# Gated cross-attention and mixture of experts on one core: SyncE's queue writes the query parts ahead of the key reads, and sends the query reads and the reciprocals ahead of the row of maxima

## What is computed

```python
q = proj(x1t, Wq, bq);  k = proj(x2t, Wk, bk);  v = proj(x2t, Wv, bv)
scores = jnp.einsum('bhqd,bhkd->bhqk', q, k) / sqrt(16)
out = jnp.einsum('bhqk,bhkd->bhqd', softmax(scores), v)
...
x = x + jnp.tanh(g_xattn[0]) * attention(_layernorm(x), ctx)
x = x + jnp.tanh(g_ffn[0]) * moe_and_shared_ffn(_layernorm(x))
```

## Time and profile before

| | us |
|---|---|
| median of 3 runs | 1412.91 |
| lowest and highest run | 1408.93, 1428.1 |
| the profiled execution | 1411.02 |
| its span (first to last instruction) | 1409.1 |
| PE busy | 1290.6 (92%) |
| DVE busy | 974.3 (69%) |
| ACT busy | 874.1 (62%) |
| POOL busy | 863.3 (61%) |
| mean granted TensorE clock, of full speed | 0.982 |

### The profile page before, as it was taken

One profiled execution on the slowest core, in us unless ns is written; L12 is line 12 of the kernel. 1 busy time (PEld: TensorE's weight loads), 2 busy tenths in 40 slices (PEclk: granted clock), 3 DMA queues, 4 the chain that ended last, 5 costly groups with the idle time before them and its releaser, 6 DMA issues.

```text
span 1409.1 us, 34589 instructions
## 1 busy us (share of the span) xinstructions
PE 1290.6 (92%) x12274; PEld 680.4 (48%) x12274; DVE 974.3 (69%) x1661; ACT 874.1 (62%) x1720; POOL 863.3 (61%) x1267
## 2 busy tenths in 40 slices
PE   2899899999998899889999988799999999999997
PEld 0233333333333333323333332387788878888885
DVE  4988889999987798888889887556654323333332
ACT  2488788888877788778878876534334333333332
POOL 8547677767787687867787752640214555555553
PEclk7799999999999999999999999999999999999999
DMA  6567777777777677677777664376654888886565
GB/s 177 166 175 212 205 215 210 206 211 193 194 207 191 187 194 197 189 187 208 192 196 193 196 164 112 122 209 145 126 176 90 203 197 202 198 190 112 111 108 80
DMA packets 161348, 248.28 MB, mean 176 GB/s; under 512 B 33733, under 2 KB 58956, under 8 KB 161182
## 3 DMA queue, kind: packets, MB, share of 16 engines
q1 hardware_dynamic: 142926, 208.70, 53.5%
q0 software_dynamic: 18256, 37.38, 14.5%
HBM read 141.06 MB, written 103.88 MB: 174 GB/s over the span
## 4 chain that ended last, share of the span: by engine, by line
PE 42%; DMA 13%; SPq 12%; issue 12%; POOL 9%; DVE 9%; ACT 2%; POOLq 1%; DVEq 0%; another core or an unknown queue 0%; ACTq 0%
PE m_banks L969 19%; SPq L471 7%; PE bank L926 6%; PE bank L895 6%; DVE row_max L1142 6%; PE m_banks L873 4%; DMA arena<-pv_d 4%; DMA arena<-parts_q 4%; DMA parts_k<-arena 3%; PE bank L901 2%; POOL xs L793 2%; SPq L532 2%; PE bank L857 1%; PE bank L851 1%; PE bank L991 1%
## 5 line engine op out<-in xcount | busy, mean ns | idle before, releaser
L1142 DVE TENSOR_REDUCE row_max<-m_banks 128x2 f32<-128x1024 f32 x512 | 614.8, 1221 | 98.5 <-PE m_banks L873 89.7
L1426 ACT ACTIVATE arena<-bank 128x512 f32<-128x512 f32 x1024 | 554.4, 605 | 97.7 <-PE bank L895 89.9
L895 PE MATMUL bank<-arena 112*32 112x512 bf16 x4096 | 338.2, 384 | 11.9 <-ACT arena L1426 7.2
L926 PE MATMUL bank<-arena 128*32 128x512 f32 x2048 | 283.2, 603 | 1.9 <-issue 1.6
L895 PEld LDWEIGHTS bank<-arena 112*32 112x32 bf16 x4096 | 113.1, 95 | 275.5 <-ACT arena L1426 136.3
L873 PE MATMUL m_banks<-arena 48*128 48x512 bf16 x1024 | 176.6, 391 | 58.2 <-DMA arena<-parts_q 29.2
L805 POOL DMA_INDIRECT out<-xs,ids x71 | 112.3, 1581 | 172.9 <-ACT xs L1508 140.7
L969 PE MATMUL m_banks<-w_ring,h_hi 128*128 x568 | 183.0, 403 | 0.0
L1497 ACT ACTIVATE arena<-m_banks 128x256 f32<-128x256 f32 x103 | 39.5, 384 | 189.7 <-PE m_banks L969 179.3
L873 PEld LDWEIGHTS m_banks<-arena 48*128 48x128 bf16 x1024 | 40.3, 94 | 194.7 <-issue 83.2
L694 POOL TENSOR_TENSOR arena<-arena 128x512 f32<-128x512 f32 x32 | 40.9, 1279 | 122.8 <-DMA arena<-pv_d 119.4
(11 more groups left out here) (182 smaller groups left out, 1997.9 us busy)
## 6 DMA issues: line engine op xcount, KB each, us to landing
pv_d<-arena SPq DMA_DIRECT2D x32, 512.0 KB, 4.4
w_ring<-split_d SPq DMA_DIRECT2D x60, 256.0 KB
parts_k<-arena SPq DMA_DIRECT2D x96, 128.0 KB
parts_q<-arena SPq DMA_DIRECT2D x96, 128.0 KB
arena<-parts_k SPq DMA_DIRECT2D x64, 192.0 KB
arena<-parts_q SPq DMA_DIRECT2D x64, 192.0 KB
arena<-in_w SPq DMA_DIRECT2D x36, 256.0 KB, 7.2
arena<-in_ctx SPq DMA_DIRECT2D x32, 256.0 KB, 3.7
```

Source lines behind the costliest of these rows:

```text
L895: last = nc.tensor.matmul(out[c, :], k_stack[b % 3][0:SHIFTED, h, kt * P + c.start:kt * P + c.stop], q_stack[b % 3][0:SHIFTED, h, :], star ...
L926: last = nc.tensor.matmul(pv_ps[2 * DH * j:2 * DH * (j + 1), :], v_ones[b % 3][:, kt, GROUP * g + j, :], probs[pair % 3][:, j, :], start=( ...
L1142: nc.vector.reduce_max(pair, m_ps[(STEPS * b + u) // 2 % M_PAIRS], AX_X).then_inc(s_mx, 1)
L1426: nc.scalar.activation(probs[group % 3][:, j, :], bank_of["scores", b, s], ACT.Exp, scale=float(DH) ** -0.5).then_inc(s_exp, 1)
```

## The change

In every turn SP now issues the writes of query MID and LO ahead of the key reads. The query reads come right behind `load_x`, then `store_reciprocals`, and `row(i+1, 0)` last, just ahead of `load_values`. No DMA is added or removed, and no wait is added or removed in the program; only the order in SP's program is another. For batch 0 (i = -2) the writes stood ahead of the key reads already.

```diff
                 if is_b(i + 2):
-                    if i + 2 > 0:
-                        read(i + 2, 0)
                     write(i + 2, 1, MID)
                     write(i + 2, 1, LO)
-                    if i + 2 == 0:
-                        read(0, 0)
+                    read(i + 2, 0)
                 if is_b(i + 4) and i + 4 >= 2:
                     load_ctx(i + 4)
                 if is_b(i - 3):
                     store_turned(i - 3)
                 if i >= 0 and is_b(i + X_AHEAD):
                     load_x(i + X_AHEAD)
+                if is_b(i + 2):
+                    read(i + 2, 1)
+                if is_b(i - 1):
+                    store_reciprocals(i - 1)
                 if is_b(i + 1):
                     row(i + 1, 0)
-                if is_b(i - 1):
-                    store_reciprocals(i - 1)
-                if is_b(i + 2):
-                    read(i + 2, 1)
                 if is_b(i - 1):
                     load_values(i - 1)
```

## The result

| | before | changed |
|---|---|---|
| median, us | 1418.76 (4 runs) | 1511.74 (4 runs) |
| lowest to highest | 1408.93 to 1428.1 | 1507.07 to 1519.58 |
| span of the profiled execution | 1409.1 | 1505.2 |

The account below looks back on a forecast made before the run. PE, ACT and DVE were taken to set the pace, 25.94 us in a quiet turn; a serial ring through POOL would make turns 27.5 us against 26.85: 1411.0 + 18 + 1.9 = 1431 us, range 1400 to 1456.

Parts of the forecast that it names:

- The new wait at the LO write: SP at L457: stands from about 263.5 until POOL has made query LO at 266.96; key reads start 3.5 us later.
- R: The time when POOL has made query LO; 266.96 us in turn 8 of the kernel before.
- The query reads: SP's reads behind load_x: start at R + 6.1, 1.7 us earlier than before, with 0 taken for their own wait.
- quiet turn: A turn in which PE hardly waits for a DMA: 25.94 us before, forecast to go to 26.5.
- The ring through POOL: From R to the next R through SP's issues, the values' landing and POOL: 14.8 + 4.6 + 7.1 = 26.5 us, all serial.
- R bound nobody: In the kernel before, query LO followed SP with 3.5 us of room and held up nothing.
- I take 3.6: SP at L498: reciprocals land 3.6 us from the end of the query reads, 1.6 us of wait a turn.
- I take 4.6: From the end of the values' load issue to POOL's start on them: 4.6 us, between 3.8 and 5.8.
- The sum: Quiet turn 26.5 us, with disturbances 27.5 a turn against 26.85; over 28 turns 18 us, giving 1431 us.
- disturbances: Added to each turn: 0.3 us for slower read issues, 0.5 for later query reads, about 0.2 for later values.
- The rivals: Stalls vanish, likelier 1398 us (chance 0.15); nothing moves, 1413 (0.17); disturbances add up, 1462 (0.23).
- The slower rival: Late query reads delay reciprocals, row and values by 2.2 us in half the turns: 28.6 a turn, 1462 us, chance 0.23.

Follow-up runs that it names:

- run 7: Changed kernel, with POOL making the query split ahead of add_attention of the turn before; ratio 1.022 to the kernel before.
- run 8: Kernel before, with POOL making the query split ahead of add_attention of the turn before; ratio 1.026 to the kernel before.
- run 6: Changed kernel, with the token and staged-weight stores and the next staged load ahead of load_values; ratio 1.085 to the kernel before.
- run 5: Changed kernel, with the 256 KB load of the values issued ahead of the wait for the reciprocals; ratio 1.034 to the kernel before.
- run 3: Changed kernel, with the reciprocals' store put back ahead of the query reads; ratio 1.031 to the kernel before.

## Why the prediction was wrong, point by point

- **The new wait at the LO write: right.** SP waits at L457 for POOL, and the wait for the key parts is gone. The key reads start at R + 0.7 (predicted 0.8).
- **The query reads: right.** R + 6.1 in the quiet turn, as predicted; no wait for the query writes. In the mean of the turns it is 6.5.
- **The ring through POOL: right, and it is the cause.** The chain of the profile runs through it, its terms in the mean are 17.4 + 6.1 + 7.1 = 30.6, and opening it takes the ratio from 1.066 to 1.022 (run 7), no more than its control has (run 8). Its POOL term was 7.1, as predicted. What failed are two terms of its sum, the landings that it took at 3.6 and 4.6 us, below.
- **"R bound nobody": not quite.** In quiet turn 8 it is so, but between 125 and 850 us of the kernel before SP waited for LO 16.2 us in 18 turns. The room that the prediction saw was thinner than 3.5 us in most turns. And it didn't see at all that SP's own program, at 21.8 us of issues and 1.7 us between them, had only 3.4 us of waits in a turn of 26.85.
- **"I take 3.6" for the landing of the reciprocals: too small.** From the end of the query reads (272.11) to `load_values` (276.79) are 4.7 us in turn 7, and 5.5 us in the mean of the 27 turns. SP's wait is 3.2 us a time, not 1.6. I had priced the landing by the query reads ahead alone, as if the small store landed with them. Windows of the changed kernel around the wait show a part that I left out (start:end, length, busy of PE, PEld, DVE, ACT, POOL, clock, DMA share, GB/s):

```profile
274.00:275.00 1.00, 0.43 (x6) 0.11 (x2) 0.96 (x4) 1.00 (x3) 1.00 (x2) 1.00 0.96 117
275.00:276.00 1.00, 0.00 (x0) 0.00 (x0) 0.09 (x2) 0.15 (x1) 0.92 (x2) 1.00 0.68 122
276.00:277.00 1.00, 0.00 (x0) 0.00 (x0) 0.00 (x0) 0.00 (x0) 0.44 (x1) 1.00 0.01 2
277.00:278.00 1.00, 0.86 (x12) 0.23 (x12) 0.00 (x0) 0.41 (x1) 0.00 (x0) 1.00 0.00 0
278.00:279.00 1.00, 1.00 (x17) 0.34 (x17) 0.86 (x1) 1.00 (x3) 0.00 (x0) 1.00 0.31 115
```

  Nearly all data have moved by 276.0, and nothing moves until after 278: the DMA engines are idle for two microseconds. For the first 0.8 us SP still waits for the store to be reported (until 276.79), then the loads just issued haven't begun. It is so in all 27 turns: from 0.5 us ahead of the first load's issue to 1 us behind it the DMA share is 0.10 at most, and in most turns 0.00. The queue is drained and started anew in every turn. The Trainium skill ("DMA: Bandwidth & Descriptors", Anatomy of one DMA) puts most of a DMA's fixed cost of about 2 us into the receipt of the last write, for DMAs that GpSimd issues. These come from SP, and of the two idle microseconds only the first 0.8 can be such a receipt, so the window doesn't test that figure. Its rule that the report of a DMA comes behind all earlier writes of the same DMA engine (Queues, rings and completion order) went the right way, but 3.6 was a floor for it, not the value.
- **"I take 4.6" for the landing of the values: too small.** It is 6.3 us in turn 7 and 6.1 in the mean, longer than the 5.8 that I had as the upper bound. I had taken the 5.8 from a quiet turn, where the mean of before was 7.0, and had taken off the query reads that were no longer in flight. But by the idle window the loads now start on empty queues more than a microsecond after SP begins to issue them. That they then share the queues with the megabyte behind them is likely, but no run took it away (run 6 put it ahead: 6.3). The 3.2 us for 512 KB that the prediction worked out from the Trainium skill are a poor guide here: the page's figure is for one DMA issued by GpSimd, these are two issued by SP, and with half the amount behind the wait it still took 4.8 us (run 5).
- **The sum.** In the quiet turn the misses are 1.1 us (landing of the reciprocals), 0.6 (query reads that took 4.39 instead of 3.75 us to issue) and 1.7 (landing of the values): 26.5 + 3.4 = 29.9, as measured. In the mean the reciprocals took 5.5 us instead of 3.6, the values 6.1 instead of 4.6, and the query reads started and were issued 0.6 us later: 4.0 us together, where I had allowed 1.0 for disturbances. That makes 30.57 against 27.5, and 27 x 3.07 = 83 us: about the whole miss (1511.74 against 1431).
- **The rivals.** The slower rival had the right sign, but with 28.6 a turn less than half of the growth (1.75 us of 3.7), and another reason: disturbed turns. Here the quiet turns are at 29.9 as well. The range ended at 1456 because I had let each landing vary alone: in the ring they add. The measured 4.7 lay inside the bounds that I gave for its landing, the 6.3 outside.
- **What I had said would show.** SP at L457 for POOL: 104 us in 60 waits, 3.5 us a turn for MID and LO together, where I said some 3, for LO alone. SP at L498: 96 us where I said 45. PE's stall moved to the row: yes. POOL's wait for the values would fall: no, it rose from 3.5 to 7.3 us, as POOL now stands still while SP goes through its part of the ring. Turns of 27 to 28 us: no, 30.57.
- **Left open.** The granted clock fell from 0.99 to 0.94 over the turns, and PE's busy time rose by 30 us. The stalls of PE are longer, and the clock stands at half of full speed (1.2 of 2.4 GHz) behind several of them, as here in the changed kernel, where PE had stood for 3.4 us until turn 7 began at 247.42:

```profile
249.00:250.00 1.00, 1.00 (x13) 0.62 (x13) 1.00 (x2) 1.00 (x2) 0.00 (x0) 0.50 0.82 283
```

  30 us over 27 turns is 1.1 us a turn. The members of the ring hardly wait for what PE makes (from 125 us to turn 30 POOL waits 10.1 us in all for ACT's HI parts, and SP 2.5 us for the maxima), so by the rows it isn't on the ring; no run tested it. Nor do I know why the part behind turn 30 took 7.5 us less.

## What to carry to other kernels

In an in-order queue, ask of each wait not only who is late behind it, but whether the thing waited for depends on something that the same queue issues later in the loop: the LO write ahead of the key reads turned slack into a closed ring through POOL, and from then on every microsecond in it counted. A store whose landing is waited for belongs ahead of the large transfers; move it last and the wait drains the queue, which costs the landing and the new start. Add up what the queue itself takes to issue in a turn, too: here it was 23.5 of 26.85 us, so the queue was close to being a ring of its own. And when a ring is opened, look for the next one before calling a wait free: the same 3 us for the reciprocals cost 3.5% in the first ring and 3% in the second.

## What the runs showed of the hardware

A 16 KB store behind 768 KB of reads was reported 4.6 us after the start of its issue (272.15 to 276.79, 5.4 us in the mean of the 27 turns), though the DMA engines had next to nothing to move for the last 0.8 us; with nothing ahead it took 2.4 us. Two loads of together 512 KB, issued on idle queues, were usable 6.1 us after the end of their issue in the mean; where one of them was issued ahead of the wait, the other was usable after 4.8 us (run 5). Behind query reads still in flight the two took 6.9 us (run 3). SP took 21.9 us of issuing for the 41 DMAs of a turn (run 7), about 0.6 us for each read of parts, with some 0.04 us from one to the next.
